# A transformer layer's attention: the value products of four query tiles cut into quarters, one in each of four steps

## The chip, the cores and the metric

The kernel runs on one core of one Trainium2 chip, all in float32. The metric is the time of one execution of the whole program on that core, in microseconds (us), lower being better. An execution has three phases behind each other: a front phase (feed-forward and projections), the attention phase, and a closing phase. The change is in the attention phase alone.

## The reference

```python
x = x + 0.5 * ffn(layernorm(x))                      # x is (8, 1024, 256)
# attention, 16 heads of 16 features, for each of the 8 * 16 = 128 pairs (batch, head):
content = (q + u_bias) @ k.T                         # (1024, 1024)
pos = relative_shift((q + v_bias) @ p.T)             # row i is shifted by an amount that depends on i
attn = softmax((content + pos) * 16 ** -0.5)
head = attn @ v                                      # (1024, 16)
x = x + concat(heads) @ Wo + bo
x = x + 0.5 * ffn(layernorm(x))
```

## The kernel before

The attention phase works on 128 **units** (a batch and a head), each of 8 **tiles** of 128 query rows by 1,024 keys: 1,024 tiles. Every engine has an instruction queue of its own, written out as `step(r, t)` for t = 0 to 15 (a **body**: 16 tiles, two units). The first and the last body are written out flat, the 62 between them are one loop whose counter is `r`. After the last body `rounds` (line 612) goes on for ten more steps, in which later stages finish their tiles. Engines meet only at semaphores, so a step has no common start; below, a step begins where TensorE starts the content strips of its tile.

What happens to tile t, by line:

- **Positional scores.** Eight steps ahead (`LEAD`), TensorE's `strips` (line 702) multiplies the positional pair into `ps_pos`; ScalarE's `copy_positional` (line 782) copies it to SBUF. SyncE's `write` (line 648) stores it in DRAM with a row pitch of 1,025, and four steps later `read_back` (line 654) loads it with a pitch of 1,024, which is the relative shift. Each is a transfer of 512 KB. `read_back` first waits until the tile behind its own has been written too. SyncE's queue also loads queries, keys and values of the next unit and stores the heads of the last one.
- **Content scores.** In step t, `strips` puts the content product into `ps_con`. There is one such buffer (two banks), so `content_room` waits for `scored` of the tile before. The content and the positional pair, on four row groups of TensorE, run side by side.
- **Sum.** VectorE's `total` (line 811) adds `ps_con` to the loaded positional scores in SBUF and takes the row minimum of the negated scaled sum; it signals `scored`. GpSimd's `less_maximum` (line 853) negates and shifts; it signals `shifted`.
- **Turning.** Two steps later, TensorE's `turn` (line 722) transposes the tile in two halves of four blocks into `ps_turn`, and ScalarE's `exponentials` (line 789) writes each half as exponentials into `prob`, a ring of two buffers of four tiles (a **quad**).
- **Value products.** `times_values` (line 733) multiplies a whole quad with the values, 32 matmuls of 128 keys, accumulated in `ps_pv`: the first half (16 matmuls, four key blocks for each of the four tiles) in the step with t % 4 = 2, the second half in the step with t % 4 = 3.
- **Heads.** VectorE's `copy_products` (t % 4 = 0, after `total`) copies `ps_pv` to `head_T`; TensorE's `turn_heads` (t % 4 = 1) transposes it into `ps_head`; VectorE's `normalise` (t % 4 = 1, after `total`) divides by the row sums. `store_head` (line 666) sends a unit's heads out in the step with t % 8 = 7.

In TensorE's queue the order of a step is: strips of content and position, then the value products or `turn_heads` if the step has any, then `turn` of tile t - 2.

The trace counts a matmul as two instructions where float32 is split, so a half of the value products shows as x32.

Of the kernel before, what the change touches and what calls it, by code (L numbers as in the profile page):

```python
# [22 lines left out]
TILES = S // P  # L23
UNITS = H * B
NT = UNITS * TILES
BODY = 2 * TILES
# [4 lines left out]
QUAD = 4  # L31
# [506 lines left out]
def attention_phase(nc, keep, a):  # L538


    with ExitStack() as ctx:
# [34 lines left out]
        class Tile:  # L576
# [12 lines left out]
            def rounds(self, n, add=0):  # L589

                return self.r * (16 * BODY // n) + 16 * (self.t // n + add)
# [20 lines left out]
        def rounds(eng, step):  # L612

            last = NT // BODY - 1
            for t in range(BODY):
                step(0, t)
            with eng.Fori(1, last) as r:
                for t in range(BODY):
                    step(r, t)
            for t in range(BODY + 10):  # L620
                step(last, t)

        score_dram = a["scores"]
# [3 lines left out]
        def _(sp):  # L627
# [64 lines left out]
            for w in range(LEAD):  # L692
                write(Tile(0, w))
                if w >= READ_LAG:
                    read_back(Tile(0, w - READ_LAG))
            rounds(sp, step)
            for k in range(2):
                sp.wait_ge(head_out[k], 16 * UNITS // 2)

        @block.tensor  # L700
        def _(pe):
            def strips(t, side, first, banks, signal):
                for n in range(2):
                    rows = slice(first + STRIP * n, first + STRIP * (n + 1))
                    ins = pe.matmul(banks[:, n, :], left[side][rows, t.i * P:(t.i + 1) * P],  # L705
                                    right[side][rows, :], start=True, stop=True)
                ins.then_inc(signal, 1)

            def content_room(t):
                if t.i == 0:  # L710
                    pe.wait_ge(q_in[t.side], t.r * 16 + 16)
                    pe.wait_ge(k_in[t.side], t.r * 16 + 16)
                if t.past(1):
                    pe.wait_ge(scored, t.count())

            def positional_room(t):
                if t.i == 0:
                    pe.wait_ge(p_ready, t.units(1, 1))
                if t.past(1):
                    pe.wait_ge(pos_copied, t.count())  # L720

            def turn(t):
                pe.wait_ge(shifted, t.count(1, 1))
                for n in range(2):
                    if t.past(1):
                        pe.wait_ge(exped, t.count(2, n - 1))
                    for j in range(4):
                        kt = 4 * n + j
                        ins = pe.transpose(ps_turn[:, n, j * P:(j + 1) * P],  # L729
                                           pos_in[:, t.slot, kt * P:(kt + 1) * P], keep["ident"][:, :])  # L730
                    ins.then_inc(turned, 1)

            def times_values(t, half):
                if half == 0:
                    pe.wait_ge(v_ready, t.units(1, 1))
                    pe.wait_ge(exped, t.count(2, 2 * QUAD))
                    if t.past(QUAD):
                        pe.wait_ge(pv_copied, t.quads())
                for kt in range(TILES // 2 * half, TILES // 2 * (half + 1)):
                    for g in range(QUAD):  # L740
                        ins = pe.matmul(ps_pv[VW * g:VW * (g + 1), :], v_aug[t.side][:, kt, :],  # L741
                                        prob[t.t // QUAD % 2][:, kt, g * P:(g + 1) * P],
                                        start=(kt == 0), stop=(kt == TILES - 1))
                if half == 1:
                    ins.then_inc(pv_mm, 1)

            def turn_heads(t):

                pe.wait_ge(pv_copied, t.quads(1))
                if t.past(QUAD):  # L750
                    pe.wait_ge(normed, t.quads())
                pe.transpose(ps_head[:, :, :].rearrange("p g v -> p (g v)"), head_T[:, :], keep["ident"][:, :])\  # L752
                    .then_inc(head_mm, 1)

            def step(r, t):
                if Tile(r, t).real():
                    content_room(Tile(r, t))
                if Tile(r, t + LEAD).real():
                    positional_room(Tile(r, t + LEAD))
                if Tile(r, t).real():  # L760
                    strips(Tile(r, t), Tile(r, t).side, 0, ps_con, con_mm)
                if Tile(r, t + LEAD).real():
                    strips(Tile(r, t + LEAD), Tile(r, t).side, 2 * STRIP, ps_pos, pos_mm)
                if t % QUAD == 2 and Tile(r, t - 6).real():
                    times_values(Tile(r, t - 6), 0)
                if t % QUAD == 3 and Tile(r, t - 7).real():
                    times_values(Tile(r, t - 7), 1)
                if t % QUAD == 1 and Tile(r, t - 9).real():
                    turn_heads(Tile(r, t - 9))
                if Tile(r, t - 2).real():  # L770
                    turn(Tile(r, t - 2))

            pe.wait_ge(cleared, 1)
            pe.wait_ge(first_in, 16)
            for t in range(LEAD):
                positional_room(Tile(0, t))
                strips(Tile(0, t), 1, 2 * STRIP, ps_pos, pos_mm)
            rounds(pe, step)

        @block.scalar  # L780
# [28 lines left out]
        @block.vector  # L809
        def _(dve):  # L810
            def total(t):

                dve.wait_ge(con_mm, t.count(1, 1))
                dve.wait_ge(read[t.slot], t.rounds(RING, 1))
                if t.past(RING):
                    dve.wait_ge(shifted, t.count(1, 1 - RING))
                dve.nop(nofuse=True)
                dve.tensor_tensor_reduce(pos_in[:, t.slot, :], ps_con[:, :, :].rearrange("p a m -> p (a m)"),  # L818
                                         pos_in[:, t.slot, :], -SCALE, 3.0e38, ALU.add, ALU.min,
                                         neg_max[:, t.slot:t.slot + 1]).then_inc(scored, 1)  # L820

            def copy_products(t):
                dve.wait_ge(pv_mm, t.quads(1))
                if t.past(QUAD):
                    dve.wait_ge(head_mm, t.quads())
                dve.tensor_copy(head_T[:, :], ps_pv[:, :]).then_inc(pv_copied, 1)  # L826

            def normalise(t):
                dve.wait_ge(head_mm, t.quads(1))
                if t.past(QUAD):  # L830
                    dve.wait_ge(normed, t.quads())
                dve.reciprocal(inverse[:, :], ps_head[:, :, DH]).then_inc(inverted, 1)
                dve.wait_ge(inverted, t.quads(1))
                if t.i == 0 and t.past(BODY):
                    dve.wait_ge(head_out[t.side], t.r * 16 + 16 * (t.unit_in_body // 2))
                q = t.i // QUAD
                dve.tensor_tensor(head[t.side][:, :].rearrange("p (t d) -> p t d", d=DH)[:, QUAD * q:QUAD * (q + 1), :],  # L837
                                  ps_head[:, :, 0:DH], inverse[:, :].unsqueeze(2).to_broadcast([P, QUAD, DH]),
                                  ALU.mult).then_inc(normed, 1)

            def step(r, t):
                if Tile(r, t).real():
                    total(Tile(r, t))
                if t % QUAD == 0 and Tile(r, t - 8).real():
                    copy_products(Tile(r, t - 8))
                if t % QUAD == 1 and Tile(r, t - 9).real():
                    normalise(Tile(r, t - 9))

            rounds(dve, step)

        @block.gpsimd
# [283 lines left out]
```

## Time and profile before

| | us |
|---|---|
| time, median of 3 runs | 3494.53 |
| lowest and highest of them | 3494.47, 3496.61 |
| time of the profiled execution | 3496.67 |
| its span, first to last instruction | 3494.9 |
| first and last content strip's sum on VectorE (start) | 337.3, 3319.98 |
| TensorE busy | 3161.2 (90%) |
| ScalarE busy | 2285.4 (65%) |
| VectorE busy | 1711.3 (49%) |
| GpSimd busy | 1330.7 (38%) |

The span lies 1.8 us below the profiled execution's own time. The attention phase is some 2,983 us of it, 85%. Busy shares are means over phases, and within attention over steps of different make-up. L705 is a line of `strips`, L729 of `turn`, L741 of `times_values`, L752 of `turn_heads`, L818 of `total`, L826 of `copy_products`, L795 of `exponentials`, L651 of `write` and L663 of `read_back`.

### The profile page before, as it was taken

Reading aid. Unit: us, or ns where it says so; the run is one execution under the profiler, and the core shown is the slowest. Engines: PE = TensorE matmul, PEld = TensorE weight load, DVE = VectorE, ACT = ScalarE, POOL = GpSimd, SP = SyncE. Lnnn points to the kernel's source line nnn. Section 1 sums busy time; section 2 is a strip of 40 time slices with the busy share of each in tenths; the row PEclk is TensorE's granted clock in tenths of the full one; section 3 lists DMA queues with packets and bytes.
Section 4 is the critical chain, followed back from the end, with each engine's and each line's share of the span. In section 5 each row is a group of like instructions: output and inputs, shape, how many; then the busy total and the mean of one; then the engine's idle time right before and its main releaser. Section 6 shows DMA issues by size and latency. Waiting matters only on the chain. (4 is left out here: it accounts for less than half of the span.)

```text
span 3494.9 us, 104304 instructions
## 1 busy us (share of the span) xinstructions
PE 3161.2 (90%) x34876; PEld 1962.1 (56%) x34876; DVE 1711.3 (49%) x3603; ACT 2285.4 (65%) x3255; POOL 1330.7 (38%) x1341
## 2 busy tenths in 40 slices
PE   8996999999999999999999999999999999999988
PEld 5662555555555555555555555555555555555577
DVE  7771444444444444444444444444444444444457
ACT  3443777777767776777777777777777777777633
POOL 2111444444444444444444444444444444444410
PEclk9996999999999999999999999999999999999999
DMA  5977999999999999999999999999999999999862
GB/s 162 296 248 246 376 380 377 379 382 380 378 376 383 379 378 379 383 380 377 378 382 377 380 377 383 381 379 378 381 379 377 379 382 378 380 375 384 332 193 98
DMA packets 433552, 1231.26 MB, mean 352 GB/s; under 512 B 48992, under 2 KB 133472, under 8 KB 433504
## 3 DMA queue, kind: packets, MB, share of 16 engines
q1 hardware_dynamic: 430000, 1229.12, 95.8%
q10 hardware_dynamic: 3504, 1.53, 0.2%
q8 instruction: 27, 0.44, 0.1%
q14 instruction: 21, 0.17, 0.0%
HBM read 617.04 MB, written 613.43 MB: 352 GB/s over the span
## 5 line engine op out<-in xcount | busy, mean ns | idle before, releaser
L818 DVE CUSTOM_DVE_ANT_0 at_pos_in<-at_ps_con,at_pos_in 128x1024 f32<-128x1024 f32 x1024 | 1254.2, 1225 | 1621.7 <-PE at_ps_con L705 1184.4
L855 POOL TENSOR_SCALAR at_pos_in<-at_pos_in,at_neg_max 128x1024 f32<-128x1024 f32 x1024 | 1149.4, 1122 | 1720.3 <-DVE at_neg_max L818 1720.3
L786 ACT ACTIVATE at_pos_out<-at_ps_pos 128x1024 f32<-128x1024 f32 x1024 | 1050.0, 1025 | 651.7 <-PE at_ps_pos L705 651.7
L705 PE MATMUL at_ps_con<-at_right,at_left 32*128 32x512 f32 x4096 | 1157.3, 641 | 262.7 <-DVE at_neg_max L818 261.4
L795 ACT ACTIVATE at_prob<-at_ps_turn 128x512 f32<-128x512 f32 x2048 | 1109.1, 596 | 277.5 <-PE at_ps_turn L729 277.4
L705 PE MATMUL at_ps_pos<-at_right,at_left 32*128 32x512 f32 x4096 | 1164.9, 645 | 28.5 <-DMA at_left<-scratch_queries 20.6
L729 PE MATMUL at_ps_turn<-keep_ident,at_pos_in 128*128 128x128 f32 x8192 | 1105.3, 278 | 0.6 <-ACT at_prob L795 0.6
L729 PEld LDWEIGHTS at_ps_turn<-keep_ident,at_pos_in 128*128 128x128 f32 x8192 | 889.7, 141 | 299.0 <-ACT at_prob L795 188.1
L741 PEld LDWEIGHTS at_ps_pv<-at_prob,at_v_aug 128*32 128x32 f32 x16384 | 416.1, 109 | 387.8 <-issue 246.7
L705 PEld LDWEIGHTS at_ps_con<-at_right,at_left 32*128 32x128 f32 x4096 | 309.5, 183 | 471.7 <-ACT at_pos_out L786 367.6
L741 PE MATMUL at_ps_pv<-at_prob,at_v_aug 128*32 128x128 f32 x16384 | 553.2, 276 | 0.8 <-issue 0.8
L705 PEld LDWEIGHTS at_ps_pos<-at_right,at_left 32*128 32x128 f32 x4096 | 308.6, 184 | 39.9 <-POOL at_v_aug L893 21.0
L752 PEld LDWEIGHTS at_ps_head<-keep_ident,at_head_T 128*128 128x128 f32 x256 | 35.3, 138 | 193.3 <-issue 192.7
L872 POOL COPY at_right<-keep_pos_keys 64x512 f32 (+1 forms) x128 | 78.0, 610 | 37.3 <-POOL at_pos_in L855 20.4
L818 DVE DVE_READ_ACCUMULATOR2_ANT at_neg_max<- 128x1 f32 x1024 | 85.1, 83 | 0.0
L752 PE MATMUL at_ps_head<-keep_ident,at_head_T 128*128 128x128 f32 x256 | 83.8, 328 | 0.4 <-DVE at_head_T L826 0.4
L382 ACT ACTIVATE fr_qk<-fr_ps_qk,keep_b_qk 128x512 f32<-128x512 f32 x64 | 64.4, 1177 | 24.9 <-PE fr_ps_qk L332 24.9
L826 DVE COPY at_head_T<-at_ps_pv 128x128 f32<-128x128 f32 x256 | 73.4, 287 | 3.6 <-PE at_ps_pv L741 3.6
L534 POOL TENSOR_TENSOR fr_scale<-fr_variance,keep_minus_half 128x4 f32<-128x4 f32 x16 | 30.6, 1912 | 116.1 <-DVE fr_variance L456 116.1
L374 ACT ACTIVATE fr_z1T<-fr_ps_a 128x1024 f32<-128x1024 f32 x16 | 16.4, 1026 | 84.1 <-PE fr_ps_a L80 84.1
L1069 POOL TENSOR_TENSOR cl_scale<-cl_variance,keep_minus_half 128x4 f32<-128x4 f32 x16 | 16.1, 1009 | 134.9 <-DVE cl_variance L1051 134.9
L837 DVE TENSOR_TENSOR at_head<-at_ps_head,at_inverse 128x64 f32<-128x64 f32 x256 | 57.6, 225 | 14.3
(90 smaller groups left out, 1296.2 us busy)
## 6 DMA issues: line engine op xcount, KB each, us to landing
scratch_scores<-at_pos_out SPq DMA_DIRECT2D x1024, 512.0 KB, 6.5
at_pos_in<-scratch_scores SPq DMA_DIRECT2D x1024, 512.0 KB, 6.8
scratch_queries<-fr_qk SPq DMA_DIRECT2D x128, 256.0 KB, 4.0
at_left<-scratch_queries SPq DMA_DIRECT2D x127, 256.0 KB, 6.3
fr_x<-in_L_attn_x_dram SPq DMA_DIRECT2D x16, 512.0 KB, 6.0
scratch_x<-fr_x_bo SPq DMA_DIRECT2D x16, 512.0 KB, 5.0
scratch_keys<-fr_qk SPq DMA_DIRECT2D x32, 256.0 KB, 5.0
scratch_values<-fr_values SPq DMA_DIRECT2D x8, 1024.0 KB, 5.8
```

Source lines behind the costliest of these rows:

```text
L382: ins = act.activation(qk[k][:, o, f, :].rearrange("p (t u g) -> p t g u", u=P // GAPS, g=GAPS), ps_qk[:, f, :].rearrange("p (t g u) -> p ...
L705: ins = pe.matmul(banks[:, n, :], left[side][rows, t.i * P:(t.i + 1) * P], right[side][rows, :], start=True, stop=True)
L729: ins = pe.transpose(ps_turn[:, n, j * P:(j + 1) * P], pos_in[:, t.slot, kt * P:(kt + 1) * P], keep["ident"][:, :])
L741: ins = pe.matmul(ps_pv[VW * g:VW * (g + 1), :], v_aug[t.side][:, kt, :], prob[t.t // QUAD % 2][:, kt, g * P:(g + 1) * P], start=(kt == 0) ...
L752: pe.transpose(ps_head[:, :, :].rearrange("p g v -> p (g v)"), head_T[:, :], keep["ident"][:, :])\
L786: act.activation(pos_out[:, t.slot, :], ps_pos[:, :, :].rearrange("p a m -> p (a m)"), ACT.Copy)\
L795: act.activation(prob[t.t // QUAD % 2][:, 4 * n:4 * n + 4, k * P:(k + 1) * P], ps_turn[:, n, :].rearrange("p (j i) -> p j i", i=P), ACT.Exp)\
L818: dve.tensor_tensor_reduce(pos_in[:, t.slot, :], ps_con[:, :, :].rearrange("p a m -> p (a m)"), pos_in[:, t.slot, :], -SCALE, 3.0e38, ALU. ...
L826: dve.tensor_copy(head_T[:, :], ps_pv[:, :]).then_inc(pv_copied, 1)
L837: dve.tensor_tensor(head[t.side][:, :].rearrange("p (t d) -> p t d", d=DH)[:, QUAD * q:QUAD * (q + 1), :], ps_head[:, :, 0:DH], inverse[:, ...
L855: pool.tensor_scalar(pos_in[:, t.slot, :], pos_in[:, t.slot, :], -1.0, neg_max[:, t.slot:t.slot + 1], ALU.mult, ALU.add).then_inc(shifted, 1)
L872: pool.tensor_copy(right[1 - u.side][P // 2:P, :], keep["pos_keys"][P // 2:P, bass.ds(u.unit() % H * HALF, HALF)]).then_inc(p_ready, 1)
```

## The change

The value products of a quad are cut in four parts of eight matmuls (two key blocks for each of the four tiles), and each step issues one. The part index is (t - 6) % 4, so the parts of the quad that begins at tile b are issued in steps b + 6 to b + 9, where the halves were in b + 6 and b + 7. `turn_heads` moves from step b + 9 to b + 10, behind part 0 of the next quad. On VectorE, `copy_products` moves from step b + 8 to b + 10 and `normalise` from b + 9 to b + 11, and both now stand ahead of `total` of their step. The waits inside these functions are the same; the signal `pv_mm` goes with the last part. `rounds` goes on for twelve steps behind the last body.

```diff
-            for t in range(BODY + 10):
+            for t in range(BODY + 12):
                 step(last, t)
...
-            def times_values(t, half):
-                if half == 0:
+            def times_values(t, part):
+
+                if part == 0:
                     pe.wait_ge(v_ready, t.units(1, 1))
                     pe.wait_ge(exped, t.count(2, 2 * QUAD))
                     if t.past(QUAD):
                         pe.wait_ge(pv_copied, t.quads())
-                for kt in range(TILES // 2 * half, TILES // 2 * (half + 1)):
+                for kt in range(TILES // QUAD * part, TILES // QUAD * (part + 1)):
...
-                if half == 1:
+                if part == QUAD - 1:
                     ins.then_inc(pv_mm, 1)
...
-                if t % QUAD == 2 and Tile(r, t - 6).real():
-                    times_values(Tile(r, t - 6), 0)
-                if t % QUAD == 3 and Tile(r, t - 7).real():
-                    times_values(Tile(r, t - 7), 1)
-                if t % QUAD == 1 and Tile(r, t - 9).real():
-                    turn_heads(Tile(r, t - 9))
+                part = (t - 6) % QUAD
+                if Tile(r, t - 6 - part).real():
+                    times_values(Tile(r, t - 6 - part), part)
+                if part == 0 and Tile(r, t - 10).real():
+                    turn_heads(Tile(r, t - 10))
...
             def step(r, t):
+                if t % QUAD == 2 and Tile(r, t - 10).real():
+                    copy_products(Tile(r, t - 10))
+                if t % QUAD == 3 and Tile(r, t - 11).real():
+                    normalise(Tile(r, t - 11))
                 if Tile(r, t).real():
                     total(Tile(r, t))
-                if t % QUAD == 0 and Tile(r, t - 8).real():
-                    copy_products(Tile(r, t - 8))
-                if t % QUAD == 1 and Tile(r, t - 9).real():
-                    normalise(Tile(r, t - 9))
```

## Rows read from the trace of the kernel before

**Rows 1.** Windows: microseconds, busy time of each engine, granted clock, DMA share, GB/s.

```profile
100.00:200.00 100.00, 100.00 (x408) 68.36 (x408) 80.34 (x207) 42.03 (x43) 19.43 (x13) 1.00 0.91 286
400.00:3200.00 2800.00, 2555.47 (x30965) 1539.95 (x30968) 1309.74 (x2644) 1975.31 (x2883) 1179.13 (x1201) 1.00 1.02 379
1829.63:1876.28 46.65, 42.59 (x517) 25.67 (x516) 21.82 (x44) 32.92 (x49) 19.64 (x21) 1.00 1.01 376
```

**Rows 2.** Windows of single steps: t = 0, 4, 5, 6, 7, 8, 9, 10 of one body.

```profile
1829.63:1832.47 2.84, 2.17 (x18) 1.18 (x17) 1.37 (x3) 2.28 (x5) 0.74 (x1) 1.00 1.06 405
1841.41:1844.14 2.73, 2.16 (x17) 1.17 (x17) 1.36 (x3) 2.25 (x5) 0.79 (x1) 1.00 1.02 351
1844.14:1846.87 2.73, 2.27 (x17) 1.28 (x18) 1.40 (x4) 2.00 (x5) 1.12 (x1) 1.00 1.03 411
1846.87:1849.98 3.11, 3.11 (x49) 1.99 (x49) 1.46 (x3) 1.86 (x4) 1.46 (x2) 1.00 1.02 393
1849.98:1853.08 3.10, 3.10 (x49) 1.98 (x49) 1.23 (x2) 2.11 (x4) 1.17 (x2) 1.00 1.03 408
1853.08:1855.85 2.77, 2.17 (x18) 1.18 (x17) 1.37 (x3) 2.21 (x5) 0.74 (x1) 1.00 0.99 385
1855.85:1858.52 2.67, 2.27 (x18) 1.28 (x18) 1.40 (x5) 1.99 (x5) 1.36 (x2) 1.00 1.00 334
1858.52:1861.62 3.10, 3.10 (x48) 1.98 (x49) 1.45 (x3) 1.91 (x4) 1.51 (x2) 1.00 0.93 269
```

**Rows 3.** Timeline of steps t = 5 and 6 (start, duration, what ended the idle time).

```profile
1843.93 0.29 DVE L826 COPY at_head_T<-at_ps_pv 128x128 f32<-128x128 f32 x1
1844.14 0.70 PE L705 MATMUL at_ps_con<-at_right,at_left 32*128 32x512 f32 x2 [0.57 <-DVE at_neg_max L818]
...
1845.21 0.33 PE L752 MATMUL at_ps_head<-keep_ident,at_head_T 128*128 128x128 f32 x1
...
1845.38 1.04 PE L729 MATMUL at_ps_turn<-keep_ident,at_pos_in 128*128 128x128 f32 x8
1845.51 1.22 DVE L818 CUSTOM_DVE_ANT_0 at_pos_in<-at_ps_con,at_pos_in 128x1024 f32<-128x1024 f32 x1 [1.29 <-POOL at_pos_in L855]
1846.29 1.08 ACT L795 ACTIVATE at_prob<-at_ps_turn 128x512 f32<-128x512 f32 x2
...
1846.66 0.08 DVE L818 DVE_READ_ACCUMULATOR2_ANT at_neg_max<- 128x1 f32 x1
...
1846.87 0.70 PE L705 MATMUL at_ps_con<-at_right,at_left 32*128 32x512 f32 x2 [0.46 <-DVE at_neg_max L818]
...
1847.94 1.08 PE L741 MATMUL at_ps_pv<-at_prob,at_v_aug 128*32 128x128 f32 x32
...
1848.95 1.09 PE L729 MATMUL at_ps_turn<-keep_ident,at_pos_in 128*128 128x128 f32 x8
1849.21 0.55 SPq L651 DMA_DIRECT2D scratch_scores<-at_pos_out  x1
...
1849.97 0.53 SPq L663 DMA_DIRECT2D at_pos_in<-scratch_scores  x1
1849.98 0.70 PE L705 MATMUL at_ps_con<-at_right,at_left 32*128 32x512 f32 x2
```

**Rows 4.** Waits between 400 and 3,200 us: total, times, longest.

```profile
PE at_ps_con L705 <- DVE at_neg_max L818: 244.5, 481, 0.7
```

**Rows 5.** DMA view of two units following each other, each in 40 equal slices.

```profile
GB/s 419 405 412 426 349 363 385 391 411 285 316 349 252 349 405 370 377 398 426 384 398 377 390 328 290 386 422 426 419 391 377 370 419 405 398 412 426 391 419 391
```

```profile
GB/s 403 396 431 388 297 297 308 342 369 344 297 275 205 247 325 396 388 438 403 424 410 396 408 403 401 427 396 417 417 388 374 360 374 403 431 410 396 388 254 304
```

**Rows 6.** Score writes, then loads, from 400 to 3,200 us: issue to landing, us.

```profile
DMA to landing us min/median/max: 4.9/6.5/8.2
```

```profile
DMA to landing us min/median/max: 5.4/6.8/8.5
```

## The prediction

> **What bounds the kernel now.** I read the window of the attention phase first: TensorE is busy 2555 of 2800 us at a granted clock of 1.00, so it is near its bound but not at it, and the 16 DMA engines show a share of 1.02 at 379 GB/s [rows 1]. The reader is to see two resources that look full, and neither may be believed before the steps are looked at one by one.
>
> A body of 16 steps takes 46.65 us [rows 1] and repeats within some hundredths. Its steps are of two kinds [rows 2]. Those with a half of the value products take 3.10 or 3.11 us, and TensorE is busy in all of it. Those without take 2.67 to 2.84 us, and TensorE is busy in 2.16 to 2.28 of it. In these it waits for VectorE, 481 times in 400 to 3200 us [rows 4], one for each step of this kind.
>
> The timeline shows the two limits [rows 3]. In the light step the strips start at 1844.14, VectorE's sum starts at 1845.51 (1.37 later) and the next strips start at 1846.87 (1.36 later): with one content buffer, strips and sum go in turn, and this loop is the 2.73 us. In the heavy step TensorE's queue is the limit: strips 1.07 (1846.87 to 1847.94), half of the value products 1.01 (to 1848.95), turning 1.03 (to 1849.98), together 3.11. So the work is unevenly dealt: heavy steps wait on TensorE while the loop has room, light ones wait on the loop while TensorE idles for about half a microsecond.
>
> **The change part by part, compute alone.** Nothing is removed or added in instructions: 32 matmuls for each quad stay 32. A quarter of the products is half of 1.01, 0.505 us. TensorE's queue in each step is then 1.07 + 0.505 + 1.03 = 2.605 us. In the step with `turn_heads` it is more by 1845.38 - 1845.21 = 0.17: 2.775 us.
>
> The loop of strips and sum stays. Its length is read from the light steps: 2.84 (t = 0), 2.73 (1, 4, 5), 2.77 (8), 2.67 (9, 12, 13) [rows 2]. I give the heavy steps the length of the light ones before them: 2.73 for t = 2, 3, 6, 7 and 2.67 for 10, 11, 14, 15. The sum is 2.84 + 2.77 + 7 x 2.73 + 7 x 2.67 = 43.41 us. The steps with `turn_heads` (2, 6, 10, 14) are TensorE's: 0.045 above the loop twice and 0.105 twice, 0.3 together. The body would take 43.7 us in place of 46.65: 2.95 less, and for 64 bodies 189 us.
>
> A price that the trace does not show is that of changing from one kind of matmul to another twice in each step, where it was in half of them. Its lower bound is nothing. The upper bound I take from the step without products: strips and turning occupy 2.16 of busy time where my two terms give 1.07 + 1.03 = 2.10 [rows 2], and I round it up to 0.1 us for a block. TensorE's step is then 2.705, and 2.875 with the heads: that adds 4 x 0.1 and, in the other steps at 2.67, 5 x 0.035, about 0.6 a body or 37 us in all. I take the lower end, since the products follow the strips without a gap in the row.
>
> **What is moved, and what hides it.** `copy_products` (0.29 us) stands ahead of `total`, but in the queue it still lies between two sums. VectorE is busy for 1.23 to 1.46 us of a step [rows 2], so there is more than a microsecond between two sums. The last part of the products ends in the step before, about 1.07 + 0.505 = 1.6 us into it, while VectorE is still in its sum; the copy does not wait. It ends about 0.1 us into its step (as now, 1843.93 + 0.29 against strips at 1844.14 [rows 3]); TensorE wants it for part 0 at 1.07. If it stood behind `total`, the products would wait for it to 2.7 + 0.3, so the place matters, and it is right. `normalise` waits for the transposed heads of the step before, ready about 1.9 us into it, before the sum there ends. Exponentials: part 0 needs those of tile t - 3, which end about 0.7 us into the step; now 1846.29 + 1.08 = 1847.37 against products at 1847.94 [rows 3]. ScalarE has 1.86 to 2.28 us of work in 2.67 to 2.84: it keeps up. The buffer of the older quad is freed two steps later than before, but still a step before its first writer. `store_head` waits for a `normalise` that now falls in its own step, but SyncE comes to it only after a write of that step, some 3 us in. All these I cost at nothing; without their cover each costs its 0.2 to 0.3 us in one of four steps, at most 75 us. The drain has two steps more with no real tile in them: nothing.
>
> **The transfers.** This is where compute and result may part. A unit moves 379 GB/s x 23.32 us = 8.84 MB [rows 1]. In 43.7 / 2 = 21.85 us that asks for 405 GB/s. In the slices of two units the rate stands mostly at 385 to 430, but once or twice in each unit it falls to 205 to 350 for one to six microseconds [rows 5]; single steps show 405, 411, 393, 408 against 351, 334, 269 [rows 2]. I call 402 the undisturbed rate. At it, a unit takes 8.84 / 402 = 22.0 us. If the dips persist in full, the unit stays at 23.3.
>
> Now the dips cost 23.32 - 22.0 = 1.3 us of a unit. Do they stay when more is asked? In the deepest the share is 0.93 at 269 GB/s, and elsewhere 1.02 and more [rows 1, 2]: partly the engines lack requests, which more eager steps would supply; partly packets are slow, which they would not. I let a third of the loss stay, 0.4 us: 22.4 us for a unit, 44.8 for a body. That is 1.85 less than now, 118 us for 64 bodies. With none of the loss it is 2.65, 170 us; with half, 22.65 and 1.35 a body, 86 us.
>
> The share of 1.02 by itself proves no saturation: the steps repeat so evenly, and each is explained so fully by TensorE or the loop, that no step now waits for a transfer. Landing has room as well. A load waits for a write issued three steps and 0.76 us (1849.21 to 1849.97) before: 3 x 2.73 + 0.76 = 8.95 us, with the longest landing at 8.2. A load must land within 4 x 2.73 + 1.37 - 3.10 = 9.2 us, with the longest at 8.5 [rows 3, 6]. The rooms are 0.75 and 0.7 us: a backlog of that size passes before anything waits.
>
> The Trainium skill (HBM Reference, Specifications) gives about 358 GB/s as a core's share of the memory, and DMA: Bandwidth & Descriptors, Specifications, the same as the limit. By that a unit could not go below an estimate of 24.7 us and the change would bring nothing. The trace does not agree: 379 GB/s over 2800 us [rows 1]. The same page of the Trainium skill has about 425 GB/s for a core that streams alone; by that a unit takes an estimated 20.8 us, and compute would decide. No run here shows a mean of 425.
>
> **Rivals.**
>
> *Compute decides* (the dips vanish or matter less). For it: an even pace of requests, and slices up to 438 GB/s [rows 5]. Against it: 405 GB/s would have to hold for 2,800 us. The time is 3496.67 - 189 = 3307.7, or 3345 with the dearer blocks.
>
> *The transfers are at their limit already.* For it: the share of 1.02 and landings of 6.5 us [rows 1, 6]. Against it: undisturbed steps above 400, and a rhythm free of transfer waits. The limit of 358 GB/s in the Trainium skill (HBM Reference, Specifications) is of this kind; the trace is above it. The steps would even out at 2.9 us and gain nothing to 60 us: 3435 to 3497. The likeliest sign would be VectorE waiting for loads in every step.
>
> *Slower: a convoy on SyncE's queue.* If a write lands later than three steps and 0.76 us after its issue, `read_back` blocks the queue, and the next write stands behind it. The step is then (landing - 0.76) / 3. It passes today's mean of 2.915 us once writes land after 9.5 us, 1.3 above the longest now. At 10 us the step is 3.08 and the time 3497 + 1024 x 0.165 = 3666. Against it: landings would fall back as soon as issue slows.
>
> *The clock.* A busier TensorE might lose its clock; but where it was busy for 100 of 100 us the granted clock was 1.00 [rows 1]. I give it no chance of its own.
>
> **How the numbers follow.** The transfers limit, with part of the dips gone: 50%, 3327 to 3425. Compute decides: 27%, 3295 to 3345. The transfers are at their limit already: 17%, 3425 to 3497, of which 5% lie within 0.2% of no change (7 us, what a measurement of this kernel can tell). Convoy or another wait that costs more than it gives: 5%; something unseen within 0.2%: 1%. The profiled execution was 2.1 us above the median, so the likeliest is 3496.67 - 118 - 2.1 = 3377, which I set at 3375. Its own range is 3327 to 3425. The range for 8 in 10 leaves out the slow cases and the upper part of the limit case: 3298 to 3455. Faster 0.89, same 0.06, slower 0.05.
>
> **What the profile will show.** All steps alike at 2.75 to 2.85 us; L741 in every step as x16, about 0.5 us from its start to the turning; hardly any wait of TensorE's strips beyond 0.2 us. If I am right on the transfers, GB/s is at 390 to 400, landings are above 7.5 us, and VectorE's sum starts later after the strips than 1.37 in part of the steps, or SyncE waits for writes. If compute decides, the body is at 43.7 us and the sum follows the strips by 1.31 to 1.47 everywhere. The prediction is wrong if a part 0 waits for `copy_products`, if a quarter costs well over 0.6 us, or if the DMA rate stays at 380.

## The result, and the profile after

| | us |
|---|---|
| before, median of 4 runs | 3495.57 (3494.47 to 3497.12) |
| after, median of 4 runs | 3532.94 (3526.73 to 3535.78) |
| ratio, with its 95% interval | 1.0104 (1.0087 to 1.0122) |

The change makes the kernel 37 us slower, 1.0%. The forecast was 3375 and faster, in a range of 3298 to 3455. The profiled execution took 3534.77 us with a span of 3533.0, 38 us over the one of before, and nearly all of it, 36.7 us, lies in the attention phase: VectorE's first sum starts at 337.88 and its last at 3357.3, that is 3019.4 us in place of 2982.7.

The windows of the kernel after, the whole phase first, then a body (t = 0 to 15), then its steps t = 0, 4, 5, 6, 7, 8, 9, 10, with the columns of [rows 1, 2]:

```profile
400.00:3200.00 2800.00, 2606.72 (x30559) 1494.39 (x30555) 1291.12 (x2605) 1998.78 (x2842) 1159.58 (x1185) 1.00 1.02 374
1807.43:1853.73 46.30, 43.98 (x516) 25.24 (x517) 21.82 (x44) 33.80 (x49) 19.58 (x21) 1.00 1.02 379
1807.43:1810.26 2.83, 2.74 (x32) 1.55 (x33) 1.23 (x2) 1.86 (x3) 0.96 (x1) 1.00 1.01 345
1818.50:1821.40 2.90, 2.74 (x33) 1.55 (x33) 1.23 (x2) 2.27 (x5) 1.12 (x1) 1.00 1.03 412
1821.40:1824.76 3.36, 2.74 (x33) 1.56 (x33) 1.36 (x3) 2.57 (x5) 1.12 (x1) 1.00 1.03 407
1824.76:1827.61 2.85, 2.85 (x33) 1.65 (x34) 1.40 (x4) 1.50 (x3) 1.12 (x1) 1.00 1.05 413
1827.61:1830.57 2.96, 2.74 (x33) 1.58 (x33) 1.46 (x3) 2.32 (x5) 1.30 (x2) 1.00 1.03 393
1830.57:1833.32 2.75, 2.74 (x32) 1.54 (x33) 1.23 (x2) 1.92 (x3) 0.94 (x1) 1.00 0.98 375
1833.32:1835.99 2.67, 2.67 (x32) 1.55 (x33) 1.36 (x3) 2.02 (x4) 1.35 (x2) 1.00 1.01 358
1835.99:1838.77 2.78, 2.78 (x34) 1.66 (x33) 1.51 (x5) 2.11 (x4) 1.18 (x2) 1.00 0.99 315
```

The heavy steps of 3.10 and the idle fifth of the light ones [rows 2] are gone. Some steps are at their floor, 2.67 to 2.78 us with TensorE busy throughout. But t = 5 takes 3.36, and the whole phase moves 374 GB/s where it moved 379 [rows 1]. This body, at 46.30 us, is a short one: from tile 160 to 960 the mean body, by the starts of VectorE's sums, is 47.29 us, against 46.65 before. The 0.64 us in 64 bodies are 41 us, near the 38 that the profiled executions lie apart.

What step t = 5 waits for is in its timeline, in the form of [rows 3]:

```profile
1821.40 0.70 PE L705 MATMUL at_ps_con<-at_right,at_left 32*128 32x512 f32 x2 [0.16 <-DVE at_neg_max L818]
...
1822.08 0.53 SPq L663 DMA_DIRECT2D at_pos_in<-scratch_scores  x1
1822.48 0.65 PE L742 MATMUL at_ps_pv<-at_prob,at_v_aug 128*32 128x128 f32 x16
1822.63 1.02 ACT L786 ACTIVATE at_pos_out<-at_ps_pos 128x1024 f32<-128x1024 f32 x1 [0.71 <-PE at_ps_pos L705]
1823.05 1.09 PE L729 MATMUL at_ps_turn<-keep_ident,at_pos_in 128*128 128x128 f32 x8
1823.39 1.22 DVE L818 CUSTOM_DVE_ANT_0 at_pos_in<-at_ps_con,at_pos_in 128x1024 f32<-128x1024 f32 x1 [2.12 <-DMA at_pos_in<-scratch_scores]
...
1824.55 0.28 DVE L826 COPY at_head_T<-at_ps_pv 128x128 f32<-128x128 f32 x1
1824.76 0.70 PE L705 MATMUL at_ps_con<-at_right,at_left 32*128 32x512 f32 x2 [0.61 <-DVE at_neg_max L818]
```

The sum starts 1.99 us after the strips, not 1.37, and the releaser is a transfer, the load of the scores. The next strips start 1.37 us after the sum, as ever. The waits of VectorE and TensorE and then of SyncE's queue, both from 400 to 3200 us:

```profile
DVE at_pos_in L818 <- DMA at_pos_in<-scratch_scores: 962.1, 585, 2.8
...
DVE at_pos_in L818 <- PE at_ps_con L705: 364.0, 239, 1.8
...
PE at_ps_con L705 <- DVE at_neg_max L818: 168.2, 365, 1.7
```

```profile
SPq L46 <- ACT at_pos_out L786: 640.3, 733, 2.5
SPq L46 <- DMA scratch_scores<-at_pos_out: 266.7, 473, 1.7
```

VectorE waits for a load in 585 of some 948 steps; before, no wait for a load and none for a write stood in these lists. The landings, from the DMA view of the same stretch (KB of one transfer, median us to landing), have grown by about 3 us over [rows 6]; the rooms for them were 8.95 and 9.2 us:

```profile
at_pos_in<-scratch_scores SPq DMA_DIRECT2D x948, 512.0 KB, 9.6
scratch_scores<-at_pos_out SPq DMA_DIRECT2D x947, 512.0 KB, 9.7
```

### The profile page after: what moved, and what is told of

The parts are those of the page before. It is cut to its first block and busy times, and to the rows that moved or that the text cites. A ratio compares the mean times of both kernels' runs of the same rounds, so it can differ in the third digit from the quotient of the medians.

```text
span 3533.0 us, 104180 instructions
## 1 busy us (share of the span) xinstructions
PE 3253.8 (92%) x34876; PEld 1936.6 (55%) x34876; DVE 1711.1 (48%) x3603; ACT 2339.2 (66%) x3255; POOL 1326.5 (38%) x1341
## 5 line engine op out<-in xcount | busy, mean ns | idle before, releaser
L742 PEld LDWEIGHTS at_ps_pv<-at_prob,at_v_aug 128*32 128x32 f32 x16384 | 385.1, 109 | 773.4 <-issue 763.4
L742 PE MATMUL at_ps_pv<-at_prob,at_v_aug 128*32 128x128 f32 x16384 | 659.3, 279 | 0.8 <-issue 0.8
```

## The experiments

Fifteen kernels ran, each beside runs of the kernel before on the same chip (medians 3495.98 to 3496.86). Ratios are to those. GB/s are bytes over time: where the bytes are the same, a lower rate and a longer time are one observation, and neither is the cause of the other.

**Is the schedule what the prediction said, and are the transfers what holds it?** Both kernels with half of each load (both leave out columns 512 to 1,023 of every load, and `pos_in` is filled with zeros once at the start):

```diff
-                sp.dma_start(pos_in[:, t.slot, :], src.rearrange("(g u c) -> u g c", g=GAPS, c=S))\
+                sp.dma_start(pos_in[:, t.slot, 0:HALF], src.rearrange("(g u c) -> u g c", g=GAPS, c=S)[:, :, 0:HALF])\
```

> The changed kernel, but each load of scores brings only the first 512 of 1,024 columns (the others keep what was there), so a step moves 0.79 MB in place of 1.05. Theory D (the transfers are at a ceiling of 375 to 380 GB/s, and the schedule itself is what the prediction said): VectorE no longer waits for loads, the body takes 43.4 to 44.1 us and the time is 3300 to 3345. Theory Q (the new order of the queues costs by itself, and late loads are its symptom): the time stays near 3530, above 3450 at the least.

> The kernel before with the same half loads. If its steps were set by TensorE and the loop of strips and sum alone, as the prediction read them, the time stays at 3495 within 3 us. If the transfers were setting it as well, it falls by more than 10.

The changed kernel took 3333.85 us, ratio 0.953 (0.9514 to 0.9546). The kernel before took 3496.02, ratio 0.9997 (0.9987 to 1.0006). In the changed one the body is 44.12 us, and VectorE waits for no load; its list of waits (400 to 3000 us) begins:

```profile
POOL at_pos_in L857 <- DVE at_neg_max L820: 1407.4, 943, 1.9
DVE at_pos_in L820 <- PE at_ps_con L707: 885.3, 649, 1.8
```

```profile
400.00:3000.00 2600.00, 2574.29 (x30408) 1486.15 (x30404) 1285.29 (x2593) 1990.86 (x2829) 1157.98 (x1179) 1.00 0.93 306
```

TensorE is busy in 99% of that window at 306 GB/s. Theory Q falls. The schedule is worth 162 us (3496.02 to 3333.85), and the kernel before was held by compute alone.

**The same without leaving anything out.** The positional scores are float16 in SBUF and DRAM between ScalarE's copy and VectorE's sum:

```diff
-        pos_out = sb("pos_out", [P, RING, S])
+        pos_out = sb("pos_out", [P, RING, S], F16)
+        loaded = sb("loaded", [P, RING, S], F16)
...
-                sp.dma_start(pos_in[:, t.slot, :], src.rearrange("(g u c) -> u g c", g=GAPS, c=S))\
+                sp.dma_start(loaded[:, t.slot, :], src.rearrange("(g u c) -> u g c", g=GAPS, c=S))\
...
-                                         pos_in[:, t.slot, :], -SCALE, 3.0e38, ALU.add, ALU.min,
+                                         loaded[:, t.slot, :], -SCALE, 3.0e38, ALU.add, ALU.min,
...
-    scratch("scores", [2, S * PITCH])
+    scratch("scores", [2, S * PITCH], F16)
```

> The changed kernel with the positional scores kept in float16 from ScalarE's copy to the sum (the rest as it was), so both big transfers have half their bytes: 0.52 MB a step. Theory D: compute alone sets the pace, as with half loads, 3320 to 3340 us. Should the narrower operand make VectorE's sum or ScalarE's copy slower, the loop of strips and sum lengthens and the time with it; if they get shorter, it falls below 3320.

> The kernel before with the positional scores in float16 from ScalarE's copy to the sum. Compute set its pace, so half the bytes of the big transfers change nothing: 3493 to 3499. The changed kernel in the same form took 3334, so the change by itself, without the ceiling, would be worth 161 us. Were the kernel before held by transfers somewhere, it gets faster by more than 10.

Changed kernel: 3333.81 us, ratio 0.9535 (0.9519 to 0.9551). Kernel before: 3496.66, ratio 1.0 (0.999 to 1.0009). The two windows say why: half the bytes leave the steps of before as they were (TensorE busy for 2556 of 2800 us, as in [rows 1]), and let those of after reach their floor. First the kernel before in this form, 400 to 3200 us, then the changed one, 400 to 3000 us, and its score transfers:

```profile
400.00:3200.00 2800.00, 2556.10 (x30995) 1540.49 (x30992) 1308.63 (x2641) 1973.67 (x2881) 1175.84 (x1201) 1.00 0.71 200
400.00:3000.00 2600.00, 2575.92 (x30431) 1486.94 (x30427) 1285.43 (x2593) 1988.69 (x2831) 1154.77 (x1180) 1.00 0.75 211
```

```profile
scratch_scores<-at_pos_out SPq DMA_DIRECT2D x1024, 256.0 KB, 3.8
at_loaded<-scratch_scores SPq DMA_DIRECT2D x1024, 256.0 KB, 3.8
```

This is the version that beats both, the kernel before by 163 us and the changed one by 199. It rounds the positional scores to 11 bits of significand, which is a change of the computation that whoever adopts it has to judge.

**Where is the ceiling, and is it one in bytes?** A load of 256 KB more for each unit in the kernel before, and 192 KB less in the changed one:

```diff
...
+                if u.past(BODY):
+                    at_once(sp, extra[u.side], u.r * 16 + 16 * (u.unit_in_body // 2))
+                sp.dma_start(spare[u.side][:, :], a["pos_rows"][0:4, :, :].rearrange("h d (e m) -> (h d e) m", e=2))\
+                    .then_inc(extra[u.side], 16)
...
```

```diff
-                rows = 2 * STRIP if u.last_unit() else P
+                rows = STRIP
```

> The kernel before with one more load of 256 KB for each unit (rows of 2 KB from a constant source, into tiles that nobody reads), 3% more bytes. Theory D: the kernel before sits just under the ceiling, so at its own pace it would need 390 GB/s and gets 375 to 380; loads come late and the time rises to 3560 to 3640. If the ceiling were at 400, as the prediction took it, the time stays at 3495 to 3500.

> The changed kernel, but the load of the next unit's queries brings 16 of its 64 rows (64 KB in place of 256, the other rows keep what they held), so a unit moves 8.65 MB in place of 8.84. Theory P (this load, into every second partition, is what makes the packets around it slow once in each unit, and is behind most of the 1.3 us that the dips cost): the dip is gone from the slices and the time falls by more than 120 us, to 3330 to 3410. Theory D alone (a flat ceiling in bytes): 2.2% less, 66 us, so 3467, with the dip in place.

Kernel before with more: 3596.45 us, ratio 1.0297 (1.0267 to 1.0328), 3% more bytes and 3% more time. Its window from 400 to 3200, and the wait that it did not have:

```profile
400.00:3200.00 2800.00, 2476.72 (x29911) 1489.22 (x29903) 1263.42 (x2548) 1905.93 (x2781) 1138.49 (x1159) 1.00 1.02 377
```

```profile
DVE at_pos_in L825 <- DMA at_pos_in<-scratch_scores: 691.9, 384, 3.1
```

So asking for 390 brought 377 in the mean. But the ceiling is not a fixed one: at first this kernel got all that it asked for. Its window of 390 to 575 us, and the landings of its writes there:

```profile
390.00:575.00 185.00, 168.96 (x2039) 101.50 (x2040) 86.02 (x175) 130.54 (x192) 78.44 (x80) 1.00 1.02 393
```

```profile
DMA to landing us min/median/max: 6.8/7.8/9.1
```

The four bodies from tile 16 to tile 79 took 46.63 to 46.65 us, as in the kernel before, at 393 GB/s and with no wait for a load. Only then do the bodies lengthen, to a mean of 48.46 us from tile 160 to 960, at 375 GB/s in the window of 1200 to 2000 us, with landings of 9.9.

The changed kernel with fewer queries: 3444.73 us, ratio 0.9849 (0.9832 to 0.9865), at 375 GB/s. That is 88 us less than the changed kernel; bytes alone gave 66 and theory P at least 120. Its profiled execution is the longest of five, 3462.11 us: a unit of 8.64 MB at 375 GB/s is 23.04 us, a body 46.1, and its mean body is 46.15. The long-run rate of 375 carries this run too, and the theory that the queries' load is behind most of the slow stretch is not borne out.

**Do the heads' small packets cause the slow stretch?** One store with 16 of 128 partitions, one with its rows in one block:

```diff
-                sp.dma_start(a["heads"][t.unit(), :, :].rearrange("(g u) n -> u g n", g=GAPS), head[t.side][:, :])\
+                sp.dma_start(a["heads"][t.unit(), 0:16, :], head[t.side][0:16, :])\
```

```diff
-                sp.dma_start(a["heads"][t.unit(), :, :].rearrange("(g u) n -> u g n", g=GAPS), head[t.side][:, :])\
+                sp.dma_start(a["heads"][t.unit(), :, :], head[t.side][:, :])\
```

> The changed kernel, but the store of a unit's heads sends 16 partitions in place of 128 (8 KB for 64 KB), and one store at the end of attention fills the rest, some 20 to 30 us. Theory H (the packets of 512 bytes that go to DRAM cause the stretch of slow packets which follows them in each unit, 0.7 to 1.3 us a unit): the attention phase is shorter by 90 to 160 us, the time 3400 to 3470 with the fill. Theory D alone: less bytes by 0.6% and 8 packets fewer for each engine and unit, 0.2 us a unit, so 25 us less, and with the fill 3530.

> The changed kernel, but heads are stored with partition p going to row p, one block of 64 KB, in place of four interleaved runs of rows (the output then has its rows in another order). Theory H with the interleaving as its cause: the time falls by 50 us or more. Otherwise no change within the scatter, 3527 to 3536.

3536.7 us (ratio 1.0113, 1.0089 to 1.0136) and 3536.67 (1.0106, 1.0089 to 1.0122). Theory D had 3530 and 3527 to 3536, so both lie a little above it, by 7 and by 1 us, and neither near theory H: with few heads the mean body is 46.86 us, 0.43 less than 47.29 and 28 us in 64 bodies, which the fill at the end takes back. Theory H falls.

**Is it asking too much, or is it the even spacing?** The changed kernel with one or two transposes more in each step:

```diff
+                    if n == 1:
+                        for _ in range((1, 2, 1, 2)[t.t % QUAD]):
+                            ins = pe.transpose(ps_turn[:, n, j * P:(j + 1) * P],
+                                               pos_in[:, t.slot, kt * P:(kt + 1) * P], keep["ident"][:, :])
                     ins.then_inc(turned, 1)
```

> The changed kernel with one or two transposes of the last block done again in each step, some 0.13 us each, six for four steps, so that TensorE alone makes the body 46.7 to 47.2 us, as long as before, while the products stay in quarters. Theory O (asking for more than the transfers can give is what costs the last 1%; asked at the pace of before they deliver what they did): 3495 to 3515, landings near 6.5 us, and hardly a wait for loads. Theory E (the even spacing, or where it places the transfers, is what they bear badly): 3530 or more, with waits for loads as in the changed kernel.

Its five executions lie far apart, 3526.18, 3466.79, 3447.53, 3516.10 and 3504.31 us, where every other kernel here stays within 23 us, so no ratio is drawn from it (for the two shortest alone it is 0.9887, 0.9855 to 0.9919). All five are below the changed kernel, 3526.73 to 3535.78, though TensorE has more to do, and two are below the kernel before. Neither theory is borne out: four of the five lie outside the 3495 to 3515 of theory O, none reaches the 3530 of theory E, and the kernel did not ask at the pace of before but faster. The floor of its schedule is at or below the shortest, 3447: I had priced a repeated transpose at 0.13 us, and it costs about 0.1. What may set them apart shows within the longest one, the only one profiled. Its windows of 400 to 550, 550 to 700 and 1200 to 2000 us:

```profile
400.00:550.00 150.00, 150.00 (x1779) 90.86 (x1771) 71.06 (x144) 114.36 (x158) 63.78 (x66) 1.00 1.02 386
550.00:700.00 150.00, 148.04 (x1739) 89.63 (x1731) 70.48 (x143) 113.34 (x156) 62.71 (x64) 1.00 1.02 380
1200.00:2000.00 800.00, 783.08 (x9153) 471.42 (x9155) 369.58 (x746) 595.16 (x815) 332.25 (x340) 1.00 1.02 375
```

The landings of its writes in the first and the last of these:

```profile
DMA to landing us min/median/max: 6.5/7.3/8.4
```

```profile
DMA to landing us min/median/max: 8.5/9.5/11.3
```

It starts free, with TensorE busy for 150 of 150 us, bodies of 45.85 us and 386 GB/s delivered. Landings grow by 2 us, the rate falls, and from 1200 us on it stays at 374 to 375. One schedule, two rates, as with the 256 KB more. That the five executions differ by how long the first one lasts would fit, but it is not shown.

**Would more room help?** `READ_LAG` 5 and 3 in the changed kernel, one line each.

> The changed kernel with READ_LAG 5: a load is issued one step later, so the write it waits for has four steps to land, and the load itself three steps less a part. If the late landings are mere delay that more room on the right side would hide, one of the two lags gains 20 us or more. If the transfers' rate is the limit, both lags stay within 10 us of 3533, or are slower, since the sum of the two rooms is the same.

> The changed kernel with READ_LAG 3: a load is issued one step earlier, has five steps less a part to land, and waits for a write issued two steps before. As for lag 5: mere delay would let one of them gain 20 us or more; a limit in rate leaves it within 10 us of 3533 or, where SyncE's queue blocks on the write, slower.

Lag 5: 3524.49 us, ratio 1.0084 (1.0067 to 1.0101), whose interval overlaps that of the changed kernel. Lag 3: 3490.46 us from ten runs, ratio 0.9986 (0.9976 to 0.9995). The first is within 10 us of 3533, the second is 42 us better, which the "limit in rate" theory did not allow. With lag 5, the phase's window, its landings and the only wait in SyncE's queue:

```profile
400.00:3200.00 2800.00, 2613.03 (x30666) 1499.64 (x30662) 1296.10 (x2614) 2006.16 (x2852) 1163.28 (x1189) 1.00 1.02 376
```

```profile
at_pos_in<-scratch_scores SPq DMA_DIRECT2D x951, 512.0 KB, 6.9
scratch_scores<-at_pos_out SPq DMA_DIRECT2D x951, 512.0 KB, 6.5
```

```profile
SPq L46 <- ACT at_pos_out L786: 873.0, 792, 2.8
```

The landings are as short as in the kernel before [rows 6] and the queue never waits for a write, and yet the rate is 376 GB/s. But a load now has a step less to land, an estimated 9.2 - 2.73 = 6.5 us, and VectorE waits for loads 443 times. So this kernel is held by the delay of its loads, and what rate the transfers could have given it is not told. With lag 3, SyncE waits more than ever for writes; its queue and then the phase's window:

```profile
SPq L46 <- DMA scratch_scores<-at_pos_out: 881.9, 745, 3.1
```

```profile
400.00:3200.00 2800.00, 2644.46 (x31035) 1518.87 (x31037) 1312.09 (x2648) 2032.06 (x2889) 1181.64 (x1203) 1.00 1.02 380
```

The rate is 380 GB/s, landings 7.4 (writes) and 6.6 us (loads). So under the ceiling the quarters are at best as good as before, within some 0.2%. The kernel before was not run with another lag.

**Is it the number of transfers in flight?** That looked likely: late and slow at 9.6 us, faster at 7. SyncE was made to hold a write back until the one three (or two) tiles before had landed, in one run a load as well:

```diff
                 at_once(sp, pos_copied, w.count(1, 1))
+                if w.past(3):
+                    v = Tile(w.r, w.t - 3)
+                    at_once(sp, written[v.slot], v.rounds(RING, 1))
```

> The changed kernel, where SyncE issues a write of scores only when the write three tiles before has landed (so at most three are in flight). Theory F (more transfers in flight lower the rate): landings of writes fall below 8.5 us, the rate rises to 377 to 381 GB/s and the time falls to 3485 to 3515. Theory R (the late landings are only the sign of a ceiling of 374 that this kernel's order has): the rate stays at 374 and the time at 3533, or is longer, since SyncE waits more.

> The same limit of three for writes and for loads. Theory F: like the limit on writes alone or a little better, 3480 to 3510. Theory R: 3533 or longer.

> At most two writes in flight. A write then has to land within two steps, 5.5 us, and the shortest landings so far are 4.9. Theory F: the rate is at 379 to 382 GB/s as long as the queue does not run dry, 3475 to 3500; if it runs dry in places, up to 3560. Theory R: 3540 or longer.

Three writes: 3532.92 us, ratio 1.0103 (1.0086 to 1.0119). Three of both: 3528.11, 1.009 (1.0067 to 1.0113). Two writes: 3660.04, 1.0465 (1.0448 to 1.0483). The DMA view and window of the first (400 to 3200 us):

```profile
at_pos_in<-scratch_scores SPq DMA_DIRECT2D x948, 512.0 KB, 8.9
scratch_scores<-at_pos_out SPq DMA_DIRECT2D x947, 512.0 KB, 8.7
```

```profile
400.00:3200.00 2800.00, 2605.26 (x30542) 1493.69 (x30541) 1291.05 (x2605) 1999.39 (x2842) 1159.39 (x1184) 1.00 1.02 374
```

Landings fell by about a microsecond, and the rate did not move. The limit of three hardly bites: from landings of 9.7 and 9.6 us and a step of 2.95, an estimated 6.5 score transfers are in flight in the changed kernel and 6.0 under the limit. With two writes in flight the rate fell to 359. So what theory F had forecast did not come in, and the form with both limits, an estimated 5.8 in flight, is at 375 GB/s. The theory itself is not excluded: by the same estimate the two free stretches above had only 5.5 (at 393 GB/s) and 5.3 (at 386, landings of 7.3 and 7.8).

**Does the place of the copies matter?** In the float16 form, so that transfers stay out of it, `copy_products` and `normalise` behind the sum of their step:

```diff
-                if t % QUAD == 2 and Tile(r, t - 10).real():
-                    copy_products(Tile(r, t - 10))
-                if t % QUAD == 3 and Tile(r, t - 11).real():
-                    normalise(Tile(r, t - 11))
                 if Tile(r, t).real():
                     total(Tile(r, t))
+                if t % QUAD == 2 and Tile(r, t - 10).real():
+                    copy_products(Tile(r, t - 10))
+                if t % QUAD == 3 and Tile(r, t - 11).real():
+                    normalise(Tile(r, t - 11))
```

> The changed kernel in float16 form (3334 us), with copy_products and normalise behind the sum of their step, as their order was before. The prediction costs the lead at nothing and says that without it part 0 waits for the copy until 2.7 + 0.3 us into its step: the step with turn_heads takes about 3.0 + 0.58 + 0.17 + 1.03 = 4.8 us in place of 2.8, 2 us for each of 256 quads, so 3800 to 3870. If VectorE's order did not matter, 3334.

3888.01 us, ratio 1.112 (1.1097 to 1.1142), 554 us over the same kernel with the copies ahead, and 18 above the expected range. The phase's window (400 to 3500 us), and TensorE's timeline, from the strips of such a step to the next:

```profile
400.00:3500.00 3100.00, 2666.51 (x30355) 1527.77 (x30354) 1283.28 (x2590) 1990.43 (x2825) 1151.23 (x1175) 0.97 0.63 176
```

```profile
1803.85 0.70 PE L707 MATMUL at_ps_con<-at_right,at_left 32*128 32x512 f32 x2
...
1806.65 0.64 PE L744 MATMUL at_ps_pv<-at_prob,at_v_aug 128*32 128x128 f32 x16 [1.66 <-DVE at_head_T L828]
1807.23 0.33 PE L755 MATMUL at_ps_head<-keep_ident,at_head_T 128*128 128x128 f32 x1
1807.39 1.04 PE L731 MATMUL at_ps_turn<-keep_ident,at_pos_in 128*128 128x128 f32 x8
1808.36 0.70 PE L707 MATMUL at_ps_con<-at_right,at_left 32*128 32x512 f32 x2
```

The products start 2.80 us after the strips in place of 1.07, and the step takes 4.51, where 4.8 was expected. The granted clock is 0.97 in the mean of this window and 1.00 in the same kernel with the copies ahead, so the 554 us are the wait and some lost clock together; the two were not separated. The lead of the copies is what lets the quarters work at all.

## Why the prediction was wrong

The step that failed is the rate in **The transfers**: "I call 402 the undisturbed rate", and then "I let a third of the loss stay". Together they make a unit of 22.4 us; measured are 23.64 (half of 47.29), and the phase moved 374 GB/s, where 395 would have been needed. The prediction's own sign of being wrong, a DMA rate that stays at 380, came in. The rest of the working holds in the main: with half the bytes the change is a gain of 162 us, against the 189 of the sum.

- **The limits of the steps before** were read rightly. Half the bytes left the kernel before at 3496 in two different ways, so no transfer set its pace.
- **Compute alone.** I had 3307.7 with products in blocks free of charge, and 3345 with the dearer blocks. The runs without the ceiling took 3334. The body is 44.12 us, where the sum said 43.7. The cheap end that I took was off: a quarter takes 0.57 us (1822.48 to 1823.05 in the timeline after), not 0.505, so the price of a block is 0.065 where the bounds were 0 and 0.1.
- **Hidden moves.** Copy, heads, exponentials and the store of heads cost nothing that shows: TensorE is busy in 99% of the phase without the ceiling. Taking the lead away costs 554 us, 2.2 us a quad against the 2 of the expectation, lost clock included.
- **The transfers.** I took the 400 GB/s of single steps for a rate that a steady demand could have, and the dips for something that demand would fill. Such rates do last for a while: with 256 KB more, 393 GB/s stood for 185 us, and with few heads, few queries or lag 3 the body of tiles 16 to 31 took 44.1 to 44.2 us. They did not last in any run. And the slow stretch still comes once in each unit of the kernel after, with landings of 9 us and more, that is with transfers always under way; two of its units in 40 slices each, as in [rows 5], the first with the DMA share of each slice in tenths:

```profile
DMA  9999998999999978999999999999999999999999
GB/s 375 290 304 411 333 297 354 355 419 409 340 340 255 248 234 326 404 411 432 404 414 414 412 416 393 421 400 415 425 397 425 404 404 418 389 389 411 418 404 354
```

```profile
GB/s 340 347 403 425 354 340 333 348 430 375 318 347 226 325 347 389 389 382 403 403 407 414 432 387 410 370 380 433 425 382 432 389 403 432 396 396 354 425 432 375
```

In its slowest slice, 234 GB/s, the engines are still busy for 70 to 80%, and in those of 255 and 248 GB/s for 90% or more, so for the larger part it is slow packets and not a lack of requests. Neither the heads' store nor, for its larger part, the queries' load is its cause. What causes it stays open. The mean with it over 2,800 us is 374 to 380 GB/s in every run here that the transfers held, the two writes in flight (359) aside. The DMA share of 1.02 [rows 1] was a warning, and I argued it away; it could not decide, since it stood there in a kernel that no transfer held.

- **The argument that misled me** is right by itself: no step of before waited for a transfer. But it says only that the demand of 379 was met. It holds no word on 405, and over a whole phase nothing above 380 was reached. I wrote "the transfers are at their limit already" as a rival, gave it 17%, and let it end at no change. Its sign came: VectorE waits for loads, in 585 of some 948 steps.
- **Past no change.** At the same rate the change would have been even. The rate is lower by 1.3%, 374 for 379 GB/s, which is the same finding as the longer time and does not explain it. Everything slower had 5% together. The convoy had part of the picture: SyncE waits for writes 473 times, and landings pass 9.5 us. But its price came from the queue's blocking. Lag 3 has 745 such waits and is faster than the changed kernel by 42 us; its landings of 7.4 us would by the same reckoning give a step of (7.4 - 0.76) / 2 = 3.32 us, and the step is 2.91. So a blocked queue does not by itself make a kernel slower than before; with at most two writes in flight (3660 us, 746 waits, landings of 5.9) it may.
- **What stays open** is why the transfers deliver 393 or 386 GB/s for some 200 us and then 375, and why the changed kernel settles at 374 where lag 3 has 380. Shown is that the fall happens within one execution of an unchanged loop, twice. As it happens landings grow by some 2 us; whether late transfers make slow ones, or the other way round, is not shown, and the number in flight is not excluded either. Shown is that lag 3 differs from lag 4 (3490 and 3533 us); lags 4 and 5 are hardly apart. Whether that is the distance in time between the write and the load of a tile, or which transfers then run side by side, was not found.

The Trainium skill (HBM Reference, Specifications) gives about 358 GB/s as a core's share when both cores of a pair stream, and about 425 for a core that streams alone. The runs that the transfers held, one core with loads and stores mixed, lie between, at 359 to 380 GB/s over 2,800 us. No run here streams in one direction, so the second figure is not tested.

## What to carry to other kernels

Before a schedule is made denser, divide the bytes of a period by the new period and ask whether any long window of the trace has ever moved that rate; single fast steps are no evidence, even 185 us at 393 GB/s were none here, and a DMA share at 1 with an unhurried rhythm means that the room is unknown, not that it is there. The cheapest way to know both answers is the pair of runs used here: halve the bytes in the old and in the new kernel. An even schedule is worth its full price only once the transfers have room, here with scores of half the width.

## What the hardware showed that was not expected

- A kernel can sit just under the rate that its transfers can hold and repeat its steps to hundredths of a microsecond: 3% more bytes cost 3% of the time (3496 to 3596 us), half the bytes change nothing. The cost does not come at once: tiles 16 to 79 still ran at the old pace, at 393 GB/s.
- One schedule can have two rates for its transfers, 386 and then 375 GB/s, with landings of 7.3 and 9.5 us (393 and 375, with 7.8 and 9.9, in the other kernel). A fixed ceiling of 375 could not have given 393 for 185 us.
- A block of products on TensorE has a fixed part. Half a set took 1.01 us (1847.94 to 1848.95 in [rows 3]) and a quarter 0.57 (1822.48 to 1823.05), so halving the block saves 0.44, and an estimated 0.13 is paid for each block, by a straight line through the two.
